# Layer 1's expert stage in straight-line code, token rows fetched four tiles at a time

## The reference, cut to what matters

```python
def _L1_ffn_ref(x, gate_w, w1, b1, w2, b2):     # s*b = 4096 tokens of h = 128, 8 experts, F = 512
    logits = x_flat @ gate_w.T
    probs = jax.nn.softmax(logits / TEMPERATURE, axis=-1)
    topk_probs, topk_idx = jax.lax.top_k(probs, TOPK)            # the best 2 of 8
    hidden = jax.nn.relu(jnp.einsum('th,ehf->tef', x_flat, w1) + b1[None])
    all_out = jnp.einsum('tef,efh->teh', hidden, w2) + b2[None]
    gathered = jnp.take_along_axis(all_out, topk_idx[:, :, None], axis=1)
    y_flat = jnp.sum(gathered * topk_probs[:, :, None], axis=1)
```

## Time and profile before

| | |
|---|---|
| median of 3 executions | 721.59 us |
| the profiled execution's own time | 724.73 us |
| its span | 723.0 us |
| first row load to last second product of the stage | 517.65 to 695.17 us |
| stage after it (read back, scale, write) | to 723 us |
| PE / DVE / ACT / POOL busy over the span | 73% / 55% / 40% / 35% |

### The profile page before, as it was taken

One profiled execution on the slowest core, in us unless ns is written; L12 is line 12 of the kernel. 1 busy time (PEld: TensorE's weight loads), 2 busy tenths in 40 slices (PEclk: granted clock), 3 DMA queues, 4 the chain that ended last, 5 costly groups with the idle time before them and its releaser, 6 DMA issues.

```text
span 723.0 us, 20905 instructions
## 1 busy us (share of the span) xinstructions
PE 526.4 (73%) x7216; PEld 420.3 (58%) x7217; DVE 400.0 (55%) x1082; ACT 291.1 (40%) x746; POOL 253.6 (35%) x303
## 2 busy tenths in 40 slices
PE   5939926778505836887888787787589999999840
PEld 3926625666402814555575475565488888888740
DVE  6477835776229575977879788787211111111117
ACT  1305722444300113436444454352055555555534
POOL 6064570665664000535234330000024343434430
PEclk8558956999956556899999999998689999999975
DMA  9998113333313300101011010000144444444539
GB/s 237 216 239 135 37 48 112 114 114 109 103 41 101 104 1 1 47 26 43 20 34 32 24 33 3 3 3 3 44 158 163 153 166 157 160 162 155 176 104 283
DMA packets 80939, 69.84 MB, mean 97 GB/s; under 512 B 8452, under 2 KB 66499, under 8 KB 80862
## 3 DMA queue, kind: packets, MB, share of 16 engines
q1 hardware_dynamic: 71696, 55.00, 27.7%
q0 software_dynamic: 6624, 12.70, 5.4%
q10 hardware_dynamic: 2542, 1.08, 0.6%
HBM read 22.66 MB, written 23.22 MB: 63 GB/s over the span
## 4 chain that ended last, share of the span: by engine, by line
PE 27%; DVE 19%; SPq 15%; issue 13%; DMA 9%; ACT 7%; POOL 7%; ACTq 1%; DVEq 0%; POOLq 0%
SPq L1109 5%; SPq L1122 4%; DMA ydram<-arena,g_id 4%; SPq L1132 3%; POOL ydram L831 3%; PE psum L558 3%; ACT arena L1518 3%; DVE arena L1649 3%; PE psum L1381 2%; ACT arena L1510 2%; PE psum L1151 2%; DMA arena<-arena 2%; PE psum L1436 2%; POOL sorted L690 2%; DVE arena L1629 2%
## 5 line engine op out<-in xcount | busy, mean ns | idle before, releaser
L690 POOL DMA_INDIRECT sorted<-xr_all,slot x96 | 95.6, 996 | 159.8 <-DVE arena L1629 121.0
L1221 POOL DMA_INDIRECT ydram<-arena,f_id x71 | 69.7, 982 | 200.2 <-DVE f_id L1197 188.0
L1182 ACT ACTIVATE arena<-psum,b1T 128x128 f32<-128x128 f32 x284 | 81.2, 368 | 78.2 <-PE psum L1151 71.7
L1205 DVE TENSOR_TENSOR arena<-psum,b_bc 128x128 f32<-128x128 f32 x71 | 20.7, 292 | 142.0 <-PE psum L1162 142.0
L1151 PE MATMUL psum<-arena 128*128 128x128 f32 x568 | 82.5, 290 | 14.1 <-DMA arena<-arena 11.2
L1151 PEld LDWEIGHTS psum<-arena 128*128 128x128 f32 x568 | 71.2, 197 | 26.6 <-issue 16.2
L1162 PE MATMUL psum<-w,arena 128*128 x568 | 80.5, 285 | 0.1
L1162 PEld LDWEIGHTS psum<-w,arena 128*128 128x128 f32 x568 | 68.8, 191 | 4.9 <-issue 1.3
L831 POOL DMA_INDIRECT ydram<-arena,g_id x40 | 43.0, 1075 | 48.6 <-DVE arena L820 22.8
L1546 ACT ACTIVATE arena<-arena 128x512 f32<-128x512 f32 x32 | 20.2, 630 | 71.9 <-DVE arena L1629 71.9
L1404 PE MATMUL psum<-arena 128*128 128x128 f32 (+3 forms) x64 | 23.4, 471 | 23.7 <-DVE arena L1666 16.8
(11 more groups left out here) (284 smaller groups left out, 1141.5 us busy)
## 6 DMA issues: line engine op xcount, KB each, us to landing
arena<-arena SPq DMA_DIRECT2D x71, 256.0 KB, 2.4
arena<-ydram SPq DMA_DIRECT2D x24, 256.0 KB, 4.2
arena<-mix SPq DMA_DIRECT2D x40, 128.0 KB
sorted<-pre_row SPq DMA_DIRECT2D x1, 4680.0 KB, 30.8
arena<-sorted SPq DMA_DIRECT2D x71, 65.0 KB, 1.9
sorted<-pre_row SPq DMA_DIRECT2D x1, 2600.0 KB, 22.1
arena<-sorted SPq DMA_DIRECT2D x10, 260.0 KB, 3.1
x_all<-in_L_attn_x_dram SPq DMA_DIRECT2D x8, 256.0 KB, 6.3
```

The source lines that it names most:

```text
L690: g.indirect_dma_start(out=dst, out_offset=bass.IndirectOffsetOnAxis(ap=slot[:, choice, t:t + 1], axis=0), in_=xr_all[:, t, :], in_offset= ...
L1182: ins = act.activation(f_hT[rr % 4][:, j * P:(j + 1) * P], psum[:, 2 + rr % 2, j * P:(j + 1) * P], ACT.Relu, bias=b1T[:, bass.ds(e * FC + ...
L1221: g.indirect_dma_start(out=ydram, out_offset=bass.IndirectOffsetOnAxis(ap=f_id[rr][:, :], axis=0), in_=f_y[rr], in_offset=None, bounds_che ...
```

## The change

The hardware loop goes: `steps` becomes a Python loop over all tiles, so that all 71 tiles are written out, tile numbers are constants and so are the waited values; the `alone` increments of the stage go. The rows are loaded four tiles in one DMA of 260 KB into one half of the same eight buffers, with one semaphore for each half; before the second use of a half SP waits once for its last tile. The lookup of the expert's number stays a register load (now from a constant address), and all copies of `w1`, products, activations, additions and scatters stay.

```diff
         RING = 8
-        f_x = [view(ROW) for _ in range(RING)]
+        FX = 4
+        f_xb = [view(FX * ROW).rearrange("p (j c) -> p j c", j=FX) for _ in range(RING // FX)]
+        f_x = [f_xb[r // FX][:, r % FX, :] for r in range(RING)]
...
-        f_ld = [sem(f"f_ld{r}") for r in range(RING)]
+        f_ld = [sem(f"f_ld{h}") for h in range(RING // FX)]
...
-        def steps(eng, lead, lag, step):
-            for k in range(-lead, RING):
-                step(k, 0, k)
-            with eng.Fori(1, NT1 // RING - 1) as i:
-                for r in range(RING):
-                    step(i * RING + r, i, r)
-            for k in range(NT1 - RING, NT1 + lag):
-                step(k, NT1 // RING - 1, k - (NT1 - RING))
+        def steps(lead, lag, step):
+            for k in range(-lead, NT1 + lag):
+                step(k)
...
+        def rows_here(eng, rr, u):
+            eng.wait_ge(f_ld[rr // FX], (u + 1) * 16)
...
         def ffn_sp(sp):
...
                     e = expert_of(sp, n)
-                    if not (isinstance(n, int) and n < 4):
+                    if n >= 4:
                         sp.wait_ge(f_hp, n - 3)
-                        alone(sp)
                     sp.dma_start(f_w1[rr % 4], w1[:, bass.ds(e, 1), :].rearrange("p a f -> p (a f)")).then_inc(
                         f_w[rr % 4], 16)
-                t = tile(k, i, r, 0)
-                if t:
-                    n, u, rr = t
-                    if not (isinstance(u, int) and u == 0):
-                        sp.wait_ge(f_xTp, n - (RING - 1))
-                        alone(sp)
-                        sp.wait_ge(f_idr, n - (RING - 1))
-                        alone(sp)
-                    sp.dma_start(f_x[rr], sv[:, bass.ds(n, 1), :].rearrange("p a c -> p (a c)")).then_inc(
-                        f_ld[rr], 16)
+                if k % FX == 0 and k < NT1:
+                    h = k // FX % 2
+                    if k >= RING:
+                        sp.wait_ge(f_xTp, k - FX)
+                        sp.wait_ge(f_idr, k - FX)
+                    sp.dma_start(f_xb[h], sv[:, k:k + FX, :]).then_inc(f_ld[h], 16)
```

More of the change, by code:

```diff
@@ L1083, in build, with tile @@
             sem(n) for n in "f_xTp f_xTr f_hp f_hTr f_yp f_yr f_idr".split())
-        f_ld = [sem(f"f_ld{r}") for r in range(RING)]
+        f_ld = [sem(f"f_ld{h}") for h in range(RING // FX)]
         f_sc = [sem(f"f_sc{r}") for r in range(RING)]
         f_w = [sem(f"f_w{r}") for r in range(4)]
-        def steps(eng, lead, lag, step):
-            for k in range(-lead, RING):
-                step(k, 0, k)
-            with eng.Fori(1, NT1 // RING - 1) as i:
-                for r in range(RING):
-                    step(i * RING + r, i, r)
-            for k in range(NT1 - RING, NT1 + lag):
-                step(k, NT1 // RING - 1, k - (NT1 - RING))
[L1101 to L1106, removed]
+        def steps(lead, lag, step):
+            for k in range(-lead, NT1 + lag):
+                step(k)
+        def tile(k, off):
+            n = k + off
+            return (n, n // RING, n % RING) if 0 <= n < NT1U else None
+        def rows_here(eng, rr, u):
+            eng.wait_ge(f_ld[rr // FX], (u + 1) * 16)
         def expert_of(eng, k):
@@ L1112, in ffn_sp, with step @@
             sv = sorted1.rearrange("(n p) c -> p n c", p=P)
-            def step(k, i, r):
-                t = tile(k, i, r, -2)
+            def step(k):
+                t = tile(k, -2)
                 if t:
@@ L1118, in step, with ffn_pe @@
                     e = expert_of(sp, n)
-                    if not (isinstance(n, int) and n < 4):
+                    if n >= 4:
                         sp.wait_ge(f_hp, n - 3)
-                        alone(sp)
                     sp.dma_start(f_w1[rr % 4], w1[:, bass.ds(e, 1), :].rearrange("p a f -> p (a f)")).then_inc(
                         f_w[rr % 4], 16)
-                t = tile(k, i, r, 0)
+                if k % FX == 0 and k < NT1:
[4 more added lines that the diff above has]
+                    sp.dma_start(f_xb[h], sv[:, k:k + FX, :]).then_inc(f_ld[h], 16)
+            steps(0, 2, step)
+        def ffn_pe(pe):
+            def step(k):
+                t = tile(k, 1)
                 if t:
                     n, u, rr = t
-                    if not (isinstance(u, int) and u == 0):
-                        sp.wait_ge(f_xTp, n - (RING - 1))
-                        alone(sp)
-                        sp.wait_ge(f_idr, n - (RING - 1))
-                        alone(sp)
-                    sp.dma_start(f_x[rr], sv[:, bass.ds(n, 1), :].rearrange("p a c -> p (a c)")).then_inc(
-                        f_ld[rr], 16)
[L1135 to L1139, removed]
-                if t:
-                    n, u, rr = t
-                    pe.wait_ge(f_ld[rr], (u + 1) * 16)
+                    rows_here(pe, rr, u)
                     pe.transpose(psum[:, rr % 2, 0:P], f_x[rr][:, 0:C], ident[:, :]).then_inc(f_xTp, 1)
-                t = tile(k, i, r, 0)
+                t = tile(k, 0)
                 if t:
@@ L1158, in step @@
                     pe.wait_ge(f_hTr, n + 1)
-                    if not (isinstance(n, int) and n < 2):
+                    if n >= 2:
                         pe.wait_ge(f_yr, n - 1)
@@ L1165, in step @@
                     mm.then_inc(f_yp, 1)
-            steps(pe, 1, 2, step)
+            steps(1, 2, step)
         def ffn_act(act):
-            def step(k, i, r):
-                t = tile(k, i, r, 1)
+            def step(k):
+                t = tile(k, 1)
                 if t:
@@ L1185, in step @@
                     ins.then_inc(f_hTr, 1)
-            steps(act, 1, 0, step)
+            steps(1, 0, step)
         def ffn_dve(v):
-            def step(k, i, r):
-                t = tile(k, i, r, 1)
+            def step(k):
+                t = tile(k, 1)
                 if t:
                     n, u, rr = t
-                    v.wait_ge(f_ld[rr], (u + 1) * 16)
-                    if not (isinstance(u, int) and u == 0):
+                    rows_here(v, rr, u)
+                    if u:
                         v.wait_ge(f_sc[rr], u * 16)
                     v.tensor_copy(f_id[rr][:, :], f_x[rr][:, C + 1:C + 2].bitcast(I32)).then_inc(f_idr, 1)
-                t = tile(k, i, r, -2)
+                t = tile(k, -2)
                 if t:
@@ L1207, in step @@
                                     ALU.add).then_inc(f_yr, 1)
-            steps(v, 1, 2, step)
+            steps(1, 2, step)
         def ffn_pool(g):
-            def step(k, i, r):
-                t = tile(k, i, r, 0)
+            def step(k):
+                t = tile(k, 0)
                 if t:
@@ L1223, in step @@
                         bounds_check=ydram.shape[0] - 1, oob_is_err=False).then_inc(f_sc[rr], 16)
-            steps(g, 0, 0, step)
+            steps(0, 0, step)
         def y0_loads(sp):
```

## The result

The changed kernel takes 687.12 us, the median of four executions (685.59 to 688.51), against 722.61 us for the kernel before on the same chip (721.18 to 726.3, four executions). The ratio is 0.9492, 95% interval 0.9453 to 0.953: faster. The prediction was 687.0 in a range of 683 to 697. The profiled execution took 685.59 us, with a span of 683.8.

The account below looks back on a forecast made before the run. SP's issue queue was taken to bound the stage, with PE's 1.896 us a tile next. Gain 33.6 - 1 + 2 = 34.6 us off the median of 721.59 gave 687.0 us, range 683 to 697.

Parts of the forecast that it names:

- What bounds the kernel: SP's issue queue sets the stage's pace, 2.456 us a tile against PE's backlog pace of 1.896; 0.56 to be had.
- Part 1: SP's issue step in the stage falls from 2.456 to 1.49 to 1.76 us, taken as 1.5, under PE's 1.896.
- Part 2: PE becomes the stage's bound, 1.896 us a tile: 131.7 us from first second product on, before 165.3; gain 33.6 us.
- Part 3: Copies of `w1` and row loads land within leads of 6.7 and 8.5 us; DMA share rises to 0.61; cost 0.
- Part 4: Register arithmetic, loop branches and `alone` increments leave all engines; gain 0 beyond SP's shorter step.
- Part 5: Written-out steps add 0.18 MB of code, 11 instruction packets; cost taken as 1 us, ends 0 and 24.
- Part 6: Stage's start and end: the second tile's products come earlier, gain 2 us (0 to 3.6); the end gives 0.
- SP in part: Rival: SP or the transfers hold the step at 2.0 us a tile; gain smaller by 7, 694 us; chance 0.17.
- Packets paid: Rival: each of 11 added instruction packets costs 2.2 us; 24 less gain, 711 us; chance 0.05.
- PE at 81 ns: Rival: PE does a pair in 81 ns, so SP's 1.5 binds; gain grows by 28, 659 us; chance 0.03.
- The exposed row load: Rival: PE stands 3.6 us for the four-tile load in each of 17 groups, 61 us; 748 us, slower; chance 0.02.

## Why the prediction was right, point by point

**What bounds the kernel** held. SP's issue was the bound, and the busy share of PE hid that there was 0.56 us a step to be had. The stretch of backlog in the earlier trace rows gave the new pace to the third digit, 1.896. That the forecast of 687.0 met 687.12 to a tenth is luck: it was taken off a median of 721.59, the four executions have 722.61, and 722.61 - 34.6 is 688.0.

**Part 1**, SP's step of 1.49 to 1.76, taken as 1.5: it is 1.47, so the taken value was right and the range missed by a hair. The upper end was too high because it took out only the load's 0.45 and one gap. The read behind the load was charged to the read. The attribution was weaker than the number: I priced the two halves as one edit and left open which of them brings SP under PE. The runs settle it. Four-tile loads alone bring it there, writing out alone does not (2.21).

**Part 2**: from the first second product to the last I had 131.7 us; it is 654.83 - 523.02 = 131.8. The 81 ns a pair of the Trainium skill ("TensorE: Matmul & The Clock Gate", section "Back-to-back issue gap") did not come about here, at the full clock. The two experiments with fewer products confirm the trace's 111.5: 1.896, 1.67 and 1.45 us a step are two pairs apart each time.

**Part 3**: the DMA share is 0.63 where I had 0.61, and PE waits for no copy in the steady part. The longest landing of a copy was 4.2 us against the lead of 6.7. The lead carries this: four or three buffers cover it, two don't, and a row load four tiles later makes the kernel slower than before.

**Part 4** named the `alone` increments as gone from all engines. POOL keeps its two a step; PE's steps are 1.896 all the same. That the loop and its register arithmetic cost nothing beyond SP was right. On SP they cost some 0.3 us a step (1.80 against 1.47), which with four-tile loads doesn't show in the time, since both are under PE's pace.

**Part 5**: 18 packets more and 0.22 MB, where I had 11 and 0.18; ten of them are of the queue whose packets are half as large. The 1 us that I set aside wasn't needed.

**Part 6** is the term that was mis-sized, by 1.3 us: from the first row load to the first second product it was 12.2 us and is 8.9, a gain of 3.3 where I took 2. The second tile's products follow the first's without a gap, at 519.79, 2.1 us after them instead of 4.4; of the rest the larger part is the clock, which is at its upper level from about 522 on instead of 530: the products just before the first second one took 1.0 instead of 1.7 us.

So the sum of 34.6 was really 33.5 (part 2) + 3.3 (part 6) = 36.8 in the profiled stage, and the medians differ by 35.5 in the first session and 37.4 in the last.

**The rivals.** SP in part: no sign of it, every step from the fourth on is 1.90. Packets paid: not in the changed kernel, where 26 packets fall into 524 to 652 us and PE waits for no copy; what they cost at a short lead isn't separated from the row loads. PE at 81 ns: no. The exposed row load: the mechanism is real, but only with the wait placed four tiles later. Its price is then 46.8 us over 16 groups, 2.9 each, where 34.6 / 16 = 2.2 turn the sign. (The prediction counted 17 groups; of 18 loads the first two wait for nothing.)

## What to carry to other kernels

When the chain names the queue that issues the transfers, read its step from stretches in which it waits for nobody and compare it with the pace at which the next engine runs off a backlog; the gain is the difference to that, however much shorter the queue's step becomes. A transfer's price on the queue isn't only its own issue: look at what the instructions right behind it take, and try another order before code is written out or transfers are merged. And when one edit does two things, run each alone: here one of them carried the whole gain.

## What the runs showed of the hardware that was not expected

A register read from SBUF on SP took 0.27 us (median) when it followed a 256 KB copy inside SBUF and 0.51 to 0.54 when it followed a 65 KB load from DRAM. That load took 0.53 to issue right behind a copy's issue and 0.34 with the register read between. Changing the order of the same instructions took 20.9 us off the kernel with one row load per tile.

With late row loads PE waited twice in each of 16 groups, 0.9 to 2.2 us for rows and 0.3 to 0.6 right after for ACT or a copy. The clock fell to 1.2 GHz behind two of these stalls (0.50 from 536 to 538 us and 0.52 from 568 to 570) and stayed at 2.4 behind the other 14, among them the longest, 2.16 us. The waits for the rows made up only half of what the late loads cost, 22.9 of 46.8 us.
